# A four-layer block in float32: the recurrence summed without a running maximum, and context rows sent through the output projection first

## What is computed

```python
# 1 attention: queries from LN(x); keys and values = 64 context rows + 64 own rows of the sequence
k = concat([ctx, LN(x) @ wk.T]);  v = concat([ctx, LN(x) @ wv.T])
x = x + tanh(g0) * (softmax(LN(x) @ wq.T @ k.T / 16) @ v) @ wo.T
# 2 gated feed-forward with ternary weights, 682 hidden
x = x + tanh(f0) * (silu(LN(x) @ w1q.T) * (LN(x) @ w3q.T)) @ w2q.T
# 3 recurrence over the 64 tokens, per channel: k = LN(x), v = ctx, decay w, bonus u, state (p, q, o)
no = max(o, u + k);    A = exp(o - no);       E = exp(u + k - no)
y = (A * p + E * v) / (A * q + E);            x = x + tanh(g1) * y
no2 = max(w + o, k);   p, q, o = exp(w+o-no2)*p + exp(k-no2)*v, exp(w+o-no2)*q + exp(k-no2), no2
# 4 experts: a shared pair of 128 columns and 8 experts of 128, weighted by the top 2 of a softmax router
x = x + tanh(f1) * (shared(LN(x)) + sum of the 2 chosen experts)
```

## Time and profile before

| | |
|---|---|
| median of 3 runs | 810.12 us (809.29 to 812.86) |
| the profiled execution | 812.55 us, span of the records 810.8 us |
| mean granted TensorE clock | 0.976 |
| middle turns | 88.7 to 90.6 us each |
| data moved by DMA | 41.25 MB, 51 GB/s |

### The profile page before, as it was taken

How to read it: one execution, slowest core, us unless ns; L and a number is a source line. 1 busy time by engine, 2 the same in 40 slices (tenths; PEclk the granted TensorE clock), 3 DMA queues, 4 the chain that set the end, 5 groups by cost and what they waited for, 6 DMA issues and landing times.

```text
span 810.8 us, 13303 instructions
## 1 busy us (share of the span) xinstructions
PE 732.4 (90%) x4620; PEld 629.0 (78%) x4620; DVE 627.2 (77%) x1034; ACT 384.4 (47%) x737; POOL 393.9 (49%) x375
## 2 busy tenths in 40 slices
PE   6988698889999899989998999989998999857896
PEld 6876697679877788778877888778877987645785
DVE  2857589687979698888979697888978797899432
ACT  3536434555455635654455635643465535422321
POOL 1014332364736465464537465455536473565264
PEclk9999969999999999999999999999999999999899
DMA  9170002010032012110031002100221000111111
GB/s 250 54 205 1 1 1 53 27 53 27 27 78 67 27 40 79 53 39 22 23 97 51 28 26 78 64 27 26 64 53 52 26 26 26 41 27 39 37 69 53
DMA packets 36208, 41.25 MB, mean 51 GB/s; under 512 B 3196, under 2 KB 27472, under 8 KB 36176
## 3 DMA queue, kind: packets, MB, share of 16 engines
q1 hardware_dynamic: 36176, 40.83, 17.3%
HBM read 36.49 MB, written 4.33 MB: 50 GB/s over the span
## 4 chain that ended last, share of the span: by engine, by line
PE 51%; DVE 20%; issue 5%; POOL 3%; ACT 2%; DMA 0%; DVEq 0%; POOLq 0%; ACTq 0%
PE sums L477 13%; PE gate_ps L477 11%; PE up_ps L477 10%; PE transit L477 7%; DVE wk L1410 3%; DVE wk L1415 3%; PE transit L542 3%; PE transit L554 3%; DVE wk L1417 2%; PE transit L469 2%; DVE act_sb L1392 2%; POOL act_sb L1150 2%; POOL hid_l L1141 2%; PE transit L522 1%; PE transit L578 1%
## 5 line engine op out<-in xcount | busy, mean ns | idle before, releaser
L1141 POOL TENSOR_TENSOR hid_l<-act_sb,hid_h 128x512 fp32r<-128x512 f32 x120 | 162.5, 1354 | 160.8 <-ACT hid_h L925 160.8
L925 ACT ACTIVATE hid_h<-act_sb 128x512 fp32r<-128x512 f32 (+1 forms) x128 | 80.4, 628 | 153.7 <-POOL act_sb L1150 120.0
L1150 POOL TENSOR_TENSOR act_sb<-act_sb,late 128x512 f32<-128x512 f32 x64 | 94.4, 1475 | 97.7 <-DVE act_sb L1394 90.2
L1392 DVE SCALAR_TENSOR_TENSOR act_sb<-act_sb,gate_ps 128x512 f32<-128x512 f32 (+1 forms) x128 | 85.9, 671 | 68.6 <-ACT act_sb L909 68.6
L477 PE MATMUL sums<-down_h,hid_h 128*128 128x256 f32 x320 | 92.9, 290 | 14.9 <-POOL hid_l L1141 14.9
L477 PE MATMUL sums<-down_l,hid_h 128*128 128x256 f32 x320 | 90.5, 283 | 0.0
L477 PE MATMUL sums<-down_h,hid_l 128*128 128x256 f32 x320 | 90.5, 283 | 0.0
L1394 DVE TENSOR_TENSOR act_sb<-act_sb,up_ps 128x512 f32<-128x512 f32 x120 | 82.4, 687 | 4.1
L477 PEld LDWEIGHTS sums<-down_h,hid_h 128*128 128x128 f32 x320 | 61.0, 191 | 22.4 <-issue 20.3
L909 ACT ACTIVATE act_sb<-gate_ps 128x512 f32<-128x512 f32 x80 | 47.2, 590 | 62.9 <-PE up_ps L477 57.6
L477 PE MATMUL gate_ps<-zm_h,gate_h 128*128 128x512 f32 x140 | 61.5, 439 | 14.2 <-DVE act_sb L1394 14.2
(11 more groups left out here) (195 smaller groups left out, 1909.1 us busy)
## 6 DMA issues: line engine op xcount, KB each, us to landing
late<-combine_rows SPq DMA_DIRECT2D x64, 256.0 KB, 3.1
ctx_tok<-in_ctx SPq DMA_DIRECT2D x8, 512.0 KB, 5.0
vals<-in_ctx SPq DMA_DIRECT2D x16, 256.0 KB, 5.7
out_x<-late SPq DMA_DIRECT2D x8, 512.0 KB, 3.2
xa<-in_x SPq DMA_DIRECT2D x7, 512.0 KB, 3.5
wk<-in_L_ffn_w SPq DMA_DIRECT2D x2, 682.0 KB
late<-in_L_ffn_w_down SPq DMA_DIRECT2D x1, 1024.0 KB, 6.9
wk<-in_L_ffn_w_gate SPq DMA_DIRECT2D x2, 512.0 KB, 4.8
```

What stands on the lines that cost most here:

```text
L925: nc.scalar.activation(hid_h[0:n, pos], act_sb[0:n, pos], ACT.Copy).then_inc(hid_h_set, 1)
L1141: nc.gpsimd.tensor_tensor(hid_l[:, pos], act_sb[:, pos], hid_h[:, pos].bitcast(F32), ALU.subtract).then_inc(hid_l_set, 1)
L1150: nc.gpsimd.tensor_tensor(act_sb[:, pos], act_sb[:, pos], comb_sb[:, pos], ALU.mult).then_inc(weighted, 1)
L1392: nc.vector.scalar_tensor_tensor(mine, mine, 1.0, gate_ps[pos][0:hidden_rows(chunk)], ALU.add, ALU.mult).then_inc(gated_one, 1)
```

## The change

Recurrence. The state is kept without a maximum. With w split in its parts below and above zero, the scans run on exp(k - max(w,0) * position) with the factor exp(min(w,0)): `key_weights` takes the exponential straight from PSUM, `keys_T` subtracts the position's part in the same accumulation (two more products with 2 rows, `grow` x `minus_pos`), `weigh_inputs` multiplies with v on GpSimd, and `scan_keys` and `scan_values` are the two sum scans. The readout is q + gamma * e and p + gamma * e * v (`add_to_sum`, `add_to_values`), with one constant `gamma` per channel. `running_max`, `exponents`, `clamps`, `decays`, `readouts`, `inputs`, `weigh_now`, `read_states` and `add_now` are gone. The remaining steps have new places in each engine's order.

Attention. wo is taken into the values ahead of the softmax: for the own rows by wv x wo, made once in turn 0 (`turn_wv`, `keep_wv`, `fuse_wv_wo`), for the context rows by `context_out` in each block, between scores and probabilities, copied into `vals` by ScalarE in four pieces. `attend` yields the projected rows at once; `project`, the copies L875 and the two DMA transfers of context values are gone. In turn 0 wo is loaded ahead of the context rows.

The core of the diff. The GpSimd, ScalarE and TensorE orders of `second` and `closing` follow the same pattern and are left out.

```diff
 TRANSIT = [
     ("A", "ctxT0"), ("A", "ctxT1"), ("M", "combT"), ("W", "z2T0"), ("W", "z2T1"), ("A", "z0T0"), ("A", "z0T1"),
-    ("A", "q0"), ("A", "q1"), ("A", "k0"), ("A", "k1"), ("A", "v0"), ("A", "v1"), ("A", "scores"), ("A", "pT"),
-    ("A", "oT0"), ("A", "oT1"), ("A", "wo0"), ("A", "wo1"), ("A", "z1T0"), ("A", "z1T1"), ("W", "yT0"), ("W", "yT1"),
+    ("A", "q0"), ("A", "q1"), ("A", "k0"), ("A", "k1"), ("A", "v0"), ("A", "v1"),
+    ("A", "scores"), ("A", "u0"), ("A", "u1"), ("A", "pT"), ("A", "wo0"), ("A", "wo1"), ("A", "z1T0"), ("A", "z1T1"), ("W", "yT0"), ("W", "yT1"),
     ("W", "z3T0"), ("W", "z3T1"), ("W", "route"), ("W", "logits"),
...
+        sp.dma_start(grow_raw, decay.partition_broadcast(2)).then_inc(consts_in, 16)
         sp.dma_start(gains[:, 0:2], g_xattn.partition_broadcast(P)).then_inc(consts_in, 16)
         sp.dma_start(gains[:, 2:4], g_ffn.partition_broadcast(P)).then_inc(consts_in, 16)
-        sp.dma_start(wo[:], woT.rearrange("(k p) e -> p k e", p=P)).then_inc(wo_in, 16)
         sp.dma_start(route_w[:, :, 0:E], router.rearrange("(k p) e -> p k e", p=P)).then_inc(route_in, 16)
...
             sp.dma_start(ctx_row, ctx_rows[t.i]).then_inc(ctx_row_in, 16)
-            sp.dma_start(vals[S:P, :, 0], ctx_seqs[t.i, 0]).then_inc(ctx_val_in, 16)
-            sp.dma_start(vals[0:S, :, 1], ctx_seqs[t.i, 1]).then_inc(ctx_val_in, 16)
...
+    def keys_T(t):
+        pe.wait_ge(z_done["W"], t.count("W", 2, 1))
+        if t.fixed and t.i == LAG["W"]:
+            pe.wait_ge(grow_set, 1)
+            pe.wait_ge(pos_set, 1)
+        for h in range(KH):
+            bank, full = claim(t, "W", f"z2T{h}")
+            for r in range(NT):
+                nc.tensor.matmul(bank[:, r * P:(r + 1) * P], zw_row[:, r, h * P:(h + 1) * P], ident[:], start=r == 0, stop=False,
+                                 is_transpose=True, skip_group_check=True)
+            nc.tensor.matmul(bank[:], grow[:, h * P:(h + 1) * P], minus_pos[:].unsqueeze(1).broadcast_to([2, NS, S]),
+                             start=False, stop=True, skip_group_check=True).then_inc(full, 1)
...
+    def fuse_wv_wo():
+        pe.wait_ge(fuse_kept, 1)
+        pe.wait_ge(wo_in, 16)
+        for k in range(KH):
+            for m in range(KH):
+                last = nc.tensor.matmul(up_ps[0][:, k * D:(k + 1) * D], wv_turned[:, m, k * P:(k + 1) * P], wo[:, m],
+                                        start=m == 0, stop=m == KH - 1)
+        last.then_inc(fuse_done, 1)
+    def context_out(t):
+        wait_taken(pe, t, "A", "ctxT0", "ctxT1", claims=("A", "u0"))
+        for pair in range(2):
+            bank, full = claim(t, "A", f"u{pair}")
+            for r in range(2):
+                for k in range(KH):
+                    for q in range(2):
+                        last = nc.tensor.matmul(bank[(1 - q) * S:(2 - q) * S, r * D:(r + 1) * D], keys[:, k, 2 * pair + r, 1 + q],
+                                                wo[:, k], start=k == 0, stop=k == KH - 1)
+            last.then_inc(full, 1)
     def scores(t):
         wait_taken(pe, t, "A", "k0", "k1", claims=("A", "scores"))
...
     def attend(t):
...
+        wait_taken(pe, t, "A", "v0", "v1", "u0", "u1", "pT", claims=("A", "wo0"))
         for pair in range(2):
             bank, full = claim(t, "A", f"wo{pair}")
             for r in range(2):
...
+                for q in range(2):
+                    tile = 2 * pair + r
+                    cols = slice((2 * tile + q) * S, (2 * tile + q + 1) * S)
+                    last = nc.tensor.matmul(bank[q * S:(q + 1) * S, r * D:(r + 1) * D], probsT[:, cols], vals[:, tile, q],
+                                            start=True, stop=True)
             last.then_inc(full, 1)
...
+            keys_T(t)
         m_up(3)
         m_down(1)
...
         m_up(5)
-        if first:
-            keep_clock(10)
+        context_out(t)
+        m_down(4)
         probs_T(t)
-        m_down(4)
         if first:
             keep_clock(3)
         attend(t)
         m_up(6)
-        if first:
-            keep_clock(3)
-        project(t)
         m_up(7)
         m_down(5)
...
         context_T(t)
-        z_T(t, "W", "z2T", zw_row, 1)
+        keys_T(t)
         scores(t)
-        keep_clock(10)
+        context_out(t)
+        keep_clock(4)
         probs_T(t)
         keep_clock(3)
         attend(t)
-        keep_clock(3)
-        project(t)
...
+    def context_out(t):
+        for pair in range(2):
+            bank = wait_full(act, t, "A", f"u{pair}")
+            for q in range(2):
+                half = slice((1 - q) * S, (2 - q) * S)
+                last = nc.scalar.activation(vals[half, 2 * pair:2 * pair + 2, q],
+                                            bank[half].rearrange("p (r d) -> p r d", r=2), ACT.Copy)
+            last.then_inc(free_of("A", f"u{pair}"), 1)
+    def key_weights(t):
+        if t.fixed and t.i == LAG["W"]:
+            act.wait_ge(scan_set, 1)
         for h in range(KH):
             bank = wait_full(act, t, "W", f"z2T{h}")
...
-            k_wide(t)
+            key_weights(t)
         normalise(t, "A", 1, xa, za_row, rstd_a, shift_a)
+        if first:
+            high("wv")
         m_chunk(3)
         high_parts(t, "A", "z0T", za_h, za_h_set)
         m_chunk(4)
         queries(t)
-        if w:
-            decays(t, 0)
         own_keys(t)
-        if w:
-            decays(t, 1)
-            readouts(t, 0)
         values(t)
         if first:
             act.wait_ge(tern_in, 64)
             act.wait_ge(low_set, SPLITS["wv"])
             nc.scalar.activation(spare2, raw2, ACT.Abs, accum_out=abs_sum[:, 2:3]).then_inc(abs_w2_set, 1)
-            act.wait_ge(consts_in, 64)
+            act.wait_ge(consts_in, 80)
             nc.scalar.activation(gains[:], gains[:], ACT.Tanh).then_inc(gains_set, 1)
+            act.wait_ge(chan_set, 1)
+            nc.scalar.activation(gamma[:], gamma[:], ACT.Exp).then_inc(chan_exp, 1)
+            nc.scalar.activation(fade[:], fade[:], ACT.Exp).then_inc(chan_exp, 1)
+            nc.scalar.activation(grow[:], grow_raw, ACT.Copy).then_inc(grow_high, 1)
         m_high(4)
         softmax(t)
         m_chunk(5, high=False)
+        context_out(t)
         probs_T(t)
-        if w:
-            readouts(t, 1)
-        attend(t)
         if first:
             high("down")
...
     def weigh_inputs(t, h):
...
+        wait_taken(pool, t, "W", f"z2T{h}")
         pool.wait_ge(vw_set, t.count("W", 1, 1))
...
+        nc.gpsimd.tensor_tensor(seqs(h, EV, 1), seqs(h, EK, 1), vw[:, h].rearrange("p (b s) -> p b s", b=NS),
                                 ALU.mult).then_inc(ev_set, 1)
...
     def low_hidden(t, chunk):
...
-            for h in range(KH):
-                inputs(t, h)
+            weigh_inputs(t, 0)
         m_low(2)
         m_weigh(3)
+        if w:
+            weigh_inputs(t, 1)
         m_low(3)
         m_weigh(4)
-        if w:
-            for h in range(KH):
-                weigh_inputs(t, h)
         m_low(4)
         m_weigh(5)
-        if w:
-            weigh_now(t, 0)
         m_low(5)
         m_weigh(6)
-        if w:
-            weigh_now(t, 1)
         m_low(6)
         row_factors(t, "A", 2, mv_a, nmean_a, var_a, rstd_a, shift_a)
         m_weigh(7)
...
+    def fade_rows():
+        dve.wait_ge(chan_exp, 2)
+        dve.wait_ge(chan_chain, 3)
         for h in range(KH):
...
+            inner = fades[:, h].rearrange("p (b s) -> p b s", b=NS)[:, :, 1:S1]
+            nc.vector.tensor_scalar(inner, inner, fade[:, h:h + 1], None, ALU.add)
+        dve.wait_ge(grow_high, 1)
+        nc.vector.tensor_tensor(grow_rest, grow_raw, grow[:].bitcast(F32), ALU.subtract).then_inc(chan_chain, 1)
+        dve.wait_ge(chan_chain, 4)
+        nc.vector.tensor_scalar(grow_raw, grow[:].bitcast(F32), ident[0:2, 0:1], None, ALU.mult).then_inc(chan_chain, 1)
+        dve.wait_ge(chan_chain, 5)
+        nc.vector.scalar_tensor_tensor(grow[:], grow_rest, ident[0:2, 1:2], grow_raw, ALU.mult, ALU.add).then_inc(grow_set, 1)
...
+    def scan_keys(t, h):
         wait_taken(dve, t, "W", f"z2T{h}")
...
+        nc.vector.tensor_tensor_scan(flat(h, QS), fades[:, h], flat(h, EK), 0.0, ALU.mult, ALU.add).then_inc(q_done, 1)
+    def scan_values(t, h):
         dve.wait_ge(ev_set, t.count("W", KH, h + 1))
...
+        nc.vector.tensor_tensor_scan(flat(h, PS), fades[:, h], flat(h, EV), 0.0, ALU.mult, ALU.add).then_inc(p_done, 1)
+    def add_to_sum(t, h):
+        dve.wait_ge(ev_set, t.count("W", KH, h + 1))
+        dve.wait_ge(q_done, t.count("W", KH, h + 1))
+        nc.vector.scalar_tensor_tensor(seqs(h, EK, 1), seqs(h, EK, 1), gamma[:, h:h + 1], seqs(h, QS, 0), ALU.mult, ALU.add).then_inc(den_set, 1)
+    def add_to_values(t, h):
+        dve.wait_ge(p_done, t.count("W", KH, h + 1))
+        nc.vector.scalar_tensor_tensor(seqs(h, EV, 1), seqs(h, EV, 1), gamma[:, h:h + 1], seqs(h, PS, 0), ALU.mult, ALU.add).then_inc(num_set, 1)
     def divide(t, h, piece):
...
```

(69 more changed lines are left out.)

227 lines of the change are left out of this document (78 added, 149 removed).

## The result

| | before | after |
|---|---|---|
| median of 20 runs each, side by side | 811.38 us | 807.93 us |
| ratio | | 0.9956, 95% interval 0.9937 to 0.9974 |
| the profiled execution's span | 810.8 us | 805.3 us |
| mean granted TensorE clock | 0.976 | 0.971 |
| VectorE, GpSimd busy | 627.2, 393.9 us | 519.6, 335.9 us |

What follows compares the result with a forecast made beforehand. TensorE was taken to bound the middle turns, VectorE the closing turn. Middle turns +2, clock +6, closing -15, turn 1 -10, turn 0 +4 make -13 us from the median 810.12: 797 us, range 776 to 819.

Steps and rivals of the forecast that it cites:

- attention's products: TensorE, middle turn: old products of 7.0 us replaced by 48 new instructions at 0.112 us, 5.4 us.
- keys_T's two products: TensorE, middle turn: two added float32r products of 512 columns at 0.23 us each, +0.47 us.
- wait ahead of attend: TensorE, middle turn: attend now waits for ScalarE's copy of the probabilities, formerly hidden by m_down(4), +0.86 us.
- the two old waits: TensorE, middle turn: waits ahead of a down product and ahead of the queries go, -3.1 us.
- wait ahead of z1T: TensorE, middle turn: a chain of 12.3 us against 8.6 us of TensorE's own work, a new wait of +3.7 us.
- clock behind it: Granted clock falls after the z1T wait: 1.5 us in five turns, less 1.6 for the old fall, +6 in all.
- turn 0: First turn: added wv x wo work, wo's load, later q_and_k and fade_rows cost +4 us (1 to 7).
- (1): New products' two halves don't overlap, 0.216 us an instruction: 830 us, slower than before; chance 0.14.
- (2): The wait ahead of z1T in the middle turns doesn't come, nor the clock's fall: 767 us; chance 0.08.
- (3): The wait ahead of z1T comes but the clock stays up: 789 us; chance 0.10.
- (4): The new attention products are as cheap as the scores, 0.056 us an instruction: 781 us; chance 0.06.
- (5): Small new waits of 1 to 3 us in each middle turn: 803 to 815 us; chance 0.14.

Runs made afterwards that it cites:

- e7: e2_attention_first with both halves' key transposes first in keys_T, then both products with 2 rows: 771.16 us.
- e3_filler: Changed kernel with 15 unneeded filler products on TensorE ahead of the z1T transposes in the middle turns: 796.61 us.
- e4_one_half: Changed kernel with all context_out products written to output rows 0 to 63, one after the other, output not the reference's: 830.86 us.
- e2_attention_first: Changed kernel with add_attention and its statistics ahead of m_gate(6) on VectorE, and GpSimd's row factors ahead of m_weigh(6): 771.11 us.
- e1_divide_first: Changed kernel with divide(0,1) and quotient(0) put back ahead of m_gate(6) on VectorE: 781.85 us.
- e6_attention_only: Kernel before with only the change's attention half, recurrence and its order as before: 832.88 us.

## Why the prediction was off

The mechanism was right and its size was not. The step that failed is the sum for a middle turn, above all two of its terms: keys_T's products and the clock. Step by step, in us for a middle turn:

| step of the prediction | forecast | measured |
|---|---|---|
| attention's products | -1.6 | -1.27 (6.76 to 5.49) |
| keys_T's two products | +0.47 | +1.17 (0.79 to 1.96) |
| wait ahead of attend | +0.86 | +0.95 (0.76 as idle) |
| the two old waits | -3.1 | -3.2 |
| wait ahead of z1T | +3.7 | +4.08 (3.92 as idle) |
| clock behind it | +1.25 (1.5 in five of six) | +1.9 (1.6 in four, 2.6 and 2.35 in the first two) |
| a turn (the one old fall of the clock left aside) | +1.6 | +3.6 by these steps, +3.4 in the trace |

Six turns less the one old fall of the clock (1.6) make +8 as forecast and +20 by the steps as measured; by the turns' starts it is the +19.0 above. Outside them: turn 0 +4 against -0.9, turn 1 -10 against -9.4, closing -15 against -14.2. The spans so differ by -5.5 us where I had -13. That the time still lies in the range is in part luck: the six turns alone missed by 11 us, and turn 0 missed by 5 us the other way.

- **keys_T**, the largest share (+0.70 a turn, 4.2 us in all): I took 0.23 us for each product with 2 rows, from products of full height that follow each other. In the trace each costs 0.43, and the four transposes ahead of the first take 0.52 and those between the two 0.59, instead of 0.40. With two transitions fewer (e7) 0.33 us came back, so a transition costs about 0.16 us by my estimate; 0.37 stayed, with two transitions left. The Trainium skill, "TensorEngine Tiling (Array Packing)", Key Properties, says that a change of the tiling mode drains TensorE; a product with 2 rows among transposes of 128 would be such a change. The 0.33 us agree with that, but no run here tells height from data type or from the transpose itself.
- **The clock**: I let it fall in five turns and priced a fall at 1.5 us. It fell in all six, and e3_filler prices it at 1.6 in four turns and at 2.6 and 2.35 in the first two, in which the half clock lasted longer. That is 11.5 us where I had 7.5, +4 us in all.
- **The wait ahead of z1T**: the chain as a whole was right within 0.2 us (12.5 from the end of m_up(6), I had 12.3), and TensorE's own work from there is 8.4 us, not 8.6. Two small errors with the same sign, +2.3 us over six turns.
- **The products**: 0.113 and 0.118 us an instruction against my 0.112, and the old ones 6.76 us from start to start rather than 7.0. +2 us.
- **Turn 0** went the other way by 5 us. The context rows' transposes came at 9.33 us, not 11.96, and the queries at 15.86, not 19.32, though wo is loaded ahead of the rows. Why they land earlier wasn't tried. The recurrence alone, with the old transfers, waited 5.7 us for them in one profile and 2.1 in another, and in the runs with the changed kernel's turn 0 the transposes came between 9.17 and 11.13 us, so this term moves by itself.

The rivals: (1), no overlap, is refuted by e4_one_half, which is also its price. The rule that I cited with it (the Trainium skill, "TensorE: Matmul & The Clock Gate", Part 3: a weight load overlaps a running matmul only where the row groups differ) doesn't hold here. Every instruction has its own weight load (PE and PEld are both x4592 on the changed kernel's page and on that of e4_one_half), those of context_out use all 128 rows, and yet e4_one_half issues one every 0.216 us, the pace of the old projection, where my estimate of the stream alone was 0.107 us per 128 columns, 0.214 for these 256. And in the two column halves the products themselves run side by side. (2), no wait, and (3), the clock stays up, didn't come; e2_attention_first and e3_filler are what they look like, at 771 and 797 us, where I had written 767 and 789. (4), 0.056 us, is refuted by the 0.113. (5), other small waits, didn't come either: its 803 to 815 us hold the time, but TensorE waits in a middle turn for nothing new beyond the two places that I named.

The prediction had a warning in its own numbers, and didn't heed it. I had a turn in which 3.1 us of waits go and 3.7 come, for which each step rests on a difference of two sums, and I gave the six turns' total no spread of its own, though 1 us in each step's difference counts six times.

## What to carry to other kernels

When work is taken out of a kernel, the order of the queues is to be looked at again. Where a product goes from TensorE, look up which chain it had covered (here the projection covered the attention sum), and move the head of that chain ahead of work that waits for something later. A wait on TensorE behind which the clock falls is to be counted at its length and once more at the clock's price (here 4.08 us and 1.65). Two halves of a change are to be timed apart, since a gain of 28 and a loss of 21 look like a change that does nothing.

## What the hardware showed that I hadn't expected

- Products with 64 columns of weights and 256 moving columns, all 128 rows shared, take 0.113 us an instruction where the two column halves alternate, and 0.220 where all go to one half (there they also all add to the same place, which e4_one_half doesn't tell apart).
- A product with 2 rows and 512 columns costs 0.43 us among transposes, 0.33 in a pair with its like; its full-height kind takes 0.23.
- Waits of 3.82 to 3.92 us brought the granted clock to 0.50 six times out of six; waits of 1.44 to 1.55 us in the same place (e1_divide_first) never did. With one wait of about 2.05 us a turn (the kernel before) it fell in one turn of six, with two of them (e6_attention_only) in four.
- The same wait cost 1.6 us behind it where the half clock was short, and 2.35 to 2.6 us where it lasted twice as long.
